# Causal masks of the score maxima: one product over all 128 rows per bank in place of four half-height products per pair of heads

## The reference, cut to what matters

```python
scores = jnp.einsum('bhqd,bhkd->bhqk', q, k) / np.sqrt(HD)
causal = jnp.triu(jnp.ones((s, s), dtype=bool), 1)
scores = jnp.where(causal[None, None], -jnp.inf, scores)   # layer 0 alone
attn_w = jax.nn.softmax(scores, axis=-1)
attn = jnp.einsum('bhqk,bhkd->bhqd', attn_w, v)
```

## Time and profile before

| what | value |
|---|---|
| median of 3 runs | 1527.2 us |
| lowest, highest | 1524.87, 1527.45 us |
| profiled execution's own time | 1526.45 us |
| its span | 1524.7 us |
| PE busy | 1369.9 us (90%), 13016 products |
| DVE busy | 1249.3 us (82%) |
| ACT busy | 1081.6 us (71%) |
| POOL busy | 278.1 us (18%) |

### The profile page before, as it was taken

One profiled execution on the slowest core, in us unless ns is written; L12 is line 12 of the kernel. 1 busy time (PEld: TensorE's weight loads), 2 busy tenths in 40 slices (PEclk: granted clock), 3 DMA queues, 4 the chain that ended last, 5 costly groups with the idle time before them and its releaser, 6 DMA issues.

```text
span 1524.7 us, 31977 instructions
## 1 busy us (share of the span) xinstructions
PE 1369.9 (90%) x13016; PEld 565.3 (37%) x13016; DVE 1249.3 (82%) x1715; ACT 1081.6 (71%) x1239; POOL 278.1 (18%) x624
## 2 busy tenths in 40 slices
PE   6699999999998768888679999999999999999886
PEld 3333434343343334446423333233333333233355
DVE  7978888888885387885989999999999999997143
ACT  6167777777777657764358888888888888887642
POOL 4021322223133132332200000000000000001252
PEclk9689999999999899999889999999999999999998
DMA  5610110101100000012120000000000000000001
GB/s 177 168 45 24 31 38 25 45 24 42 27 4 3 1 1 0 1 65 82 42 64 23 23 24 23 14 17 18 23 23 23 23 23 23 3 3 3 1 15 42
DMA packets 38995, 47.90 MB, mean 31 GB/s; under 512 B 11072, under 2 KB 20160, under 8 KB 38720
## 3 DMA queue, kind: packets, MB, share of 16 engines
q1 hardware_dynamic: 38416, 45.31, 10.1%
q10 hardware_dynamic: 432, 0.53, 0.1%
HBM read 30.22 MB, written 15.47 MB: 30 GB/s over the span
## 4 chain that ended last, share of the span: by engine, by line
PE 62%; DVE 23%; ACT 6%; issue 4%; POOL 3%; SPq 1%; DMA 1%; POOLq 0%; ACTq 0%; DVEq 0%
PE ps L426 22%; DVE l_negp L324 14%; PE ps L404 12%; PE ps L383 12%; PE ps L552 7%; ACT shared L296 3%; PE ps L443 2%; PE ps L389 2%; POOL n_rs L514 2%; DVE n_bst L495 2%; PE ps L545 1%; PE ps L1040 1%; SPq L113 1%; PE ps L908 1%; PE ps L560 1%
## 5 line engine op out<-in xcount | busy, mean ns | idle before, releaser
L324 DVE TENSOR_REDUCE l_negp<-ps 128x2 f32<-128x1024 f32 (+2 forms) x832 | 953.3, 1181 | 75.5 <-PE ps L389 36.4
L296 ACT ACTIVATE shared<-ps 128x1024 f32<-128x1024 f32 (+1 forms) x832 | 820.4, 991 | 196.8 <-PE ps L404 168.1
L426 PE MATMUL ps<-shared,l_vs 128*32 128x256 f32 (+3 forms) x6648 | 515.3, 386 | 4.1 <-POOL shared L280 3.3
L383 PE MATMUL ps<-Ks,Qs 48*128 48x512 bf16 (+3 forms) x1792 | 329.9, 369 | 40.6 <-DVE l_negp L324 27.2
L404 PE MATMUL ps<-Qs,Ks 51*128 51x512 bf16 (+3 forms) x1792 | 320.8, 366 | 25.5 <-ACT shared L296 10.7
L404 PEld LDWEIGHTS ps<-Qs,Ks 51*128 51x128 bf16 x1792 | 81.3, 93 | 330.6 <-issue 159.3
L426 PEld LDWEIGHTS ps<-shared,l_vs 128*32 128x32 f32 x6648 | 134.8, 108 | 172.3 <-issue 141.7
L383 PEld LDWEIGHTS ps<-Ks,Qs 48*128 48x128 bf16 x1792 | 87.6, 94 | 194.3 <-ACT shared L296 91.0
L280 POOL TENSOR_SCALAR_AFFINE_SELECT shared<-shared 128x512 f32<-128x512 f32 x128 | 81.7, 639 | 321.0 <-ACT shared L296 320.9
L265 POOL CAST l_parts<-l_negm 128x16 bf16<-128x16 f32 x64 | 12.6, 197 | 441.8 <-DVE l_negm L329 438.6
L389 PE MATMUL ps<-mask,id 64*128 64x128 bf16 x1024 | 69.2, 223 | 0.0
(11 more groups left out here) (160 smaller groups left out, 1090.4 us busy)
## 6 DMA issues: line engine op xcount, KB each, us to landing
Qs<-scr_q SPq DMA_DIRECT2D x128, 64.0 KB
Ks<-scr_k SPq DMA_DIRECT2D x64, 96.0 KB
Qs<-scr_q SPq DMA_DIRECT2D x128, 32.0 KB
Ks<-scr_k SPq DMA_DIRECT2D x64, 64.0 KB
scr_q<-own SPq DMA_DIRECT2D x4, 768.0 KB, 3.6
scr_q<-shared SPq DMA_DIRECT2D x4, 768.0 KB, 3.5
scr_k<-own SPq DMA_DIRECT2D x4, 768.0 KB, 5.0
scr_k<-shared SPq DMA_DIRECT2D x4, 768.0 KB, 4.8
```

The lines of the kernel that those rows point to most:

```text
L296: act.activation(dst, src, ACT.Exp, scale=SCALE).then_inc(exped, 1)
L324: dve.tensor_reduce(dst, src, AX_X, ALU.max, negate=True).then_inc(reduced, 1)
L383: last = pe.matmul(outs[par], Qs[s][r:r + MROW, h2, qt * P:(qt + 1) * P], Ks[s][r:r + MROW, h2, at:at + w], start=True, stop=True)
L426: last = pe.matmul(pv_ps[q % 2][32 * h:32 * h + 32, a:a + wide], vs[g % 2][:, kt, h, :], pT[m % PRING][:, h, a:a + wide], start=m == u.fir ...
```

## The change

The mask is added once per bank and unit. The stationary operand is the whole identity (`ident_bf`, 128 rows), the moving one the whole mask (`mask_neg`, 128 rows, repeated for both pairs of heads where they share the bank, so 256 columns). It comes after the score products of all pairs of the unit. `mask2`, `id2`, the eight DMAs and the wait for `halved` are gone.

```diff
-            if entry[1] == 0:
-                pe.wait_ge(halved, 8 * 16)
             slot_free(pe, entry)
             to = slot(entry)
             for i, h2 in enumerate(pairs):
@@
-                if causal and at + w == (qt + 1) * P:
-                    for j in range(2):
-                        for par in range(2):
-                            r = ROWS * par
-                            last = pe.matmul(outs[par][:, w - P:w], id2[r:r + ROWS, j, :], mask2[r:r + ROWS, j, :],
-                                             start=False, stop=True, skip_group_check=True)
+            if causal and at + w == (qt + 1) * P:
+                n = len(pairs)
+                for par in range(2):
+                    cut = to[:, par, 0:n * w].rearrange("p (h k) -> p h k", h=n)[:, :, w - P:w]
+                    last = pe.matmul(cut, ident_bf, mask_neg.unsqueeze(1).to_broadcast([P, n, P]),
+                                     start=False, stop=True, skip_group_check=True)
             last.then_inc(scored, 1)
...
-                sp.wait_ge(cut_out, 2)
-                sp.wait_ge(id_ready, 1)
-                for par in range(2):
-                    for j in range(2):
-                        for to, of in ((mask2, mask_neg), (id2, ident_bf)):
-                            sp.dma_start(to[ROWS * par:ROWS * (par + 1), j, :], of[ROWS * j:ROWS * (j + 1), :])\
-                                .then_inc(halved, 16)
```

More of the change, by code:

```diff
@@ L169, in order, with attention @@
         return [(t - start, e) for t, e in sorted(out, key=lambda x: (x[0], kinds.index(x[1][0]), x[1][1:]))]
-def attention(nc, ctx, all_units, place, scr, scr_m, slots, loaded, handed, v_tm, attn_tm, ident, mask2, id2, ident_bf,
-              halved, pT, ps):
+def attention(nc, ctx, all_units, place, scr, scr_m, slots, loaded, handed, v_tm, attn_tm, ident, mask_neg, ident_bf,
+              pT, ps):
     PRING, MCOLS = 4, GH * CT
@@ L1136, in two_layer_kernel @@
         mask_neg = sb("mask_neg", [P, P], BF16)
-        mask2, id2 = sb("mask2", [P, 2, P], BF16), sb("id2", [P, 2, P], BF16)
         consts = [sb(n, [P, QT]) for n in ("eps", "neg_half", "zero")]
@@ L1157, in two_layer_kernel @@
         bank = [ps[:, 2 * b * BANK:2 * (b + 1) * BANK] for b in range(B)]
-        w_first_in, w_in, small_in, blank, cut_out, id_ready, halved, consts_set, lin_added = (sem(n) for n in (
-            "w_first_in w_in small_in blank cut_out id_ready halved consts_set lin_added").split())
+        w_first_in, w_in, small_in, blank, cut_out, id_ready, consts_set, lin_added = (sem(n) for n in (
+            "w_first_in w_in small_in blank cut_out id_ready consts_set lin_added").split())
         x_in = [sem(f"x_in{b}") for b in range(B)]
@@ L1176, in two_layer_kernel @@
             nc, ctx, units, program, (scr[0:2], scr[2:4]), scr_m, slots, loaded, handed, v_tm, attn_tm, ident[:, :],
-            mask2, id2, ident_bf[:, :], halved, pT, ps)
+            mask_neg[:, :], ident_bf[:, :], pT, ps)
         def free_for(of):
```

## The result

The changed kernel takes 1538.64 us, median of 4 runs (1537.33 to 1539.30), against 1527.08 us before (4 runs, 1524.87 to 1527.45). The ratio is 1.008, with a 95% interval of 1.0065 to 1.0095: 0.8% slower. The forecast was 1541 us. The two profiled executions took 1526.45 and 1539.30 us, 12.85 us apart, and their spans are 12.9 us apart. One execution of the kernel of experiment 5 took 2318.83 us, far from all others, and is left out of the median and the ratio given there.

What follows compares the result with a forecast made beforehand. PE was taken as nearest to the bound, with 72% of the causal stretch's chain; 9.7 us (one-pair units) plus 4.8 us (both pairs) gave +14.5 us on 1526.45, so 1541 us, range 1532 to 1549 us.

Steps and rivals of the forecast that it cites:

- The products cost the same, whatever their number: Causal layer's masks: 1024 products become 384, streaming stays 0.11 us for one pair of heads; both pairs win some 0.01 us.
- A third form costs a change more: Masked units before weighing: halves to full, full to 128 x 32, two changes instead of one, 0.095 us more.
- five pairs of forms in other places: Five passages between array forms read from the trace before, from which a price of 0.09 to 0.12 us was taken.
- The rival that it might be free: Full array to 128 x 32, masks to weighing, drains nothing: 1528 to 1529 us, not slower; chance 9%.
- The price of one: Added cost per masked unit on the chain: 0.095 us with one pair of heads, 0.085 with both.
- The count: Masked units on the causal layer's chain of waits: 159, 102 with one pair of heads and 57 with both.
- The twelfth unit: Masked unit at 261.91 us in each period: PE then waits for ACT's 1.03 us exponential, so it costs nothing.
- 9 of 11 units continue on PE without a wait: Masked units on one period's chain: behind 9 PE goes on to weighing; used as argument against the waits absorbing the cost.
- The rival of absorption: Waits of PE for DVE and ACT take up perhaps half the added cost: 1531 to 1535 us; chance 7%.
- Exposed weights: Second mask product's identity load can't hide under the first: 8 to 16 us more, 1549 to 1557 us; chance 9%.
- The other signs: Profile after: PE's share of the chain should rise, and the second layer take the same time, only later.
- The DMAs and the start: Removing eight DMAs and their wait is worth nothing; before 87 us DVE's work hides added changes, else at most 7 us.

Runs made afterwards that it cites:

- experiment 5: Full-height masks only in units with both pairs of heads (4 of 12 in a group), all others as in the kernel before: 1533.04 us, ratio 1.0033.
- Runs 1: The changed kernel with its moved and widened masks kept half-height (64 rows), the eight DMAs staying: 1527.87 us against 1528.11 before, ratio 0.9999.
- run 2: The changed kernel's full-height masks, with the identity cut into four stationary operands of 32 columns: 1532.37 us against 1528.11 before, ratio 1.0022.
- run 4: Kernel before, with the full-height mask only in the last query block's first pair of heads: 1528.91 us, ratio 1.0003; period 26.88 us.
- run 3: Kernel before, with the full-height mask only in the last query block's second pair of heads: 1528.73 us against 1528.81, ratio 0.9997; period 26.78 us.

## Why the prediction was right, and where its sum was off

- **The products cost the same, whatever their number: right.** The streaming time of a unit stays what it was. Runs 1 and 2 have 768 and 1536 products, and both periods are within 0.11 us of before.
- **A third form costs a change more: right.** It was worked out from five pairs of forms in other places. The fifth, weighing to full array, showed only that the distance is the same whichever form follows, not that anything is lost. The single products of the kernel before do show a loss: a second round of weighing products is followed after 0.33 us by another form (262.36 to 262.69 us), but a round is followed after 0.216 us by more weighing (265.32 to 265.54 us), so 0.11 us is lost. The pair that no row had shown, full array to 128 x 32, now shows 0.11 us [after, 256.28 to 256.50]. The rival that it might be free is out.
- **The price of one: a little low.** 0.095 was taken for one pair, 0.085 for both. Measured are 0.107 (run 4; 0.10 in five units of the whole change) and 0.095 (run 5). The difference is the hundredth by which the second product of a run starts late; the prediction named this as a risk and left it out of its sum.
- **The count: too high, and this is the step that failed.** "So 159 units lie on it", 11 of 12 per period. By periods 9 arrive: 4 x 0.095 + 5 x 0.10 = 0.88 us, against 0.886 measured. The twelfth unit, at 261.91 us, was rightly taken for free. Two more are free that the prediction put on the chain. One is shown by run 3. The other is read from the traces alone, and no run isolates it: the scores at 252.92 us before stand 4.96 us later in the changed kernel (257.88), and those at 256.61 us again 4.96 us later (261.57), though a masked unit lies between (253.09 us before, 258.14 after). Its cost has gone into the waits ahead of the scores in this stretch (below). 7 x 0.095 + 4 x 0.085 = 1.0 us had been forecast; times 14.3 that is 14.4 us, and 0.886 x 14.3 = 12.7 us came, of 12.85 in all.
- **Luck in the total.** The two errors have opposite signs: two units too many are 2.7 us, a price too low is 1.0 us, and so 14.4 is only 1.7 us above 12.7. The forecast also stood on the profiled execution, 0.75 us under the median. 1541 us looks 0.15% off, but the forecast change of 14.5 us is 13% above that of the profiled pair (12.85) and 25% above that of the medians (11.56).
- **Why the chain misled.** The prediction read "9 of 11 units continue on PE without a wait" off a chain that showed one product behind the other. These are pieces of it, scores of 512 columns both:

```profile
256.65 0.34 PE ps L383 x2
...
258.00 0.22 PE ps L383 x2
```

Two at once stream 0.213 us. The lower piece is that and no more; the upper one holds 0.12 us of waiting, for an exponential, which the chain doesn't name: a product counts as busy until it has left the array (0.39 us for the 0.213 us of 512 columns, 256.61 us before), and that covers a wait of this size. The trace has the wait all the same, in the queue of the weight loads: the loads of the scores at 256.61 us stand 0.2 us for ACT's exponential of 255.53 us, 1.02 us long. After the change, the chain's piece for the same scores, and the piece at the place of run 3, four products of 128 columns (two rounds of 0.055 us):

```profile
261.72 0.24 PE ps L381 x2
...
264.34 0.23 PE ps L381 x4
```

The upper one has shrunk from 0.34 to 0.24 us: a mask's 0.10 us went into the wait. (A wait before it took up the same 0.10 us at 254.21 us and gave it back at the next scores, so one unit is free in this stretch, not two.) The lower one still hides 0.12 us of waiting. Such pieces must be compared with their columns before a delay is called unabsorbed.
- **The rival of absorption, 7%,** named the right mechanism and too large a share: 2 of 11 units, not half of the cost.
- **Exposed weights, 9%: out.** The two masks of a unit and the change behind them take 0.22 us together, 0.01 more than four halves did, and the second mask starts 0.066 us after the first, not over 0.1.
- **The other signs: right.** From 87 to 471 us PE's share of the chain rises from 72% to 76%, the masks' from 6.5% to 11.2%, and the second layer takes the same time (turns at 764.47 and 1404.12 us before, at 777.28 and 1416.95 us after: 639.65 and 639.67 us).
- **The DMAs and the start: right.** The first masked unit starts at 47.7 us, before at 47.5, and at the turn of maxima at 111.33 us before, the changed kernel was only 0.35 us late.

## What to carry to other kernels

On TensorE count the changes between forms of the array, not the products: rows in halves, 32-column strips and the full array don't mix freely, and each passage cost about 0.1 us here, on whatever the chain is. Put a small product into the form that its neighbour has, and let the loss fall behind the result that somebody waits for, not ahead of it. Before a delay is multiplied by a number of places, compare each start-to-start distance with its columns, since short waits hide inside a product's duration; a single edited place and the period of a repeating stretch then tell 0.01 us where totals can't tell 1.5.

## What the runs showed of the hardware that was not expected

- A change of form costs nearly the same, 0.09 to 0.12 us here, for every pair of the three forms seen: halves to full array (0.10 at 256.28 us after), full array to 128 x 32 (256.35 to 256.50 us less 0.053, 0.10), full array to halves (0.12), halves to 128 x 32 (0.09 to 0.10), and out of 128 x 32 (0.11, above). It is so with bfloat16 on both sides and with float32 on one.
- The second round after a change of form starts late, by more with float32: the second bfloat16 mask 0.066 us after the first for 0.053 us of columns (after, 256.28 us), the second round of weighing 0.240 us after the first (before, 262.12 us) where it is 0.216 with no change ahead (run 2, 254.83 us), the second float32 turn 0.164 us after the first where the next ones follow at 0.109 (before, 252.11 us).
- bfloat16 masks of 128 x 32 ahead of float32 weighing of the same form cost 0.02 us or less at the seam, and the weighing then gets to the next form in 0.53 us (254.83 to 255.36, run 2) in place of 0.57, so the number type is no change of form.
